# Codebook levels by masks and predicated copies in a transformer block: ScalarE makes the masks, VectorE picks the levels

## The reference

```
lora_delta = lora_B @ lora_A * 0.5                  # 512 x 512, rank 64
cb         = codebook / max|codebook|               # 8 levels
wg         = (weight + lora_delta) / scale          # scale = exp(scale_log), one per row and group of 128
idx        = searchsorted((cb[:-1] + cb[1:]) / 2, wg, side='left')
w_eff      = cb[idx] * scale + lora_delta
h = x @ w_eff.T
q, k, v = split(h @ Wqkv + bqkv)                    # 128 columns each
x = x + softmax(q k^T / sqrt(128)) v @ Wo + bo
base   = x @ W.T ;  logits = x @ Wr.T + 5 * onehot(language)
gates  = softmax of the top 2 of 8 logits
lora   = sum over experts of gate * (x @ A_e.T) @ B_e.T
x = x + (base + 2 * lora) @ (ffn_scale * (qweight - zero_point)).T + bias
```

## Time and profile before

| | before |
|---|---|
| median of three runs | 127.43 us (126.71, 127.43, 127.72) |
| profiled execution, first to last instruction (its span) | 125.8 us |
| TensorE busy | 104.7 us, 83% of the span |
| VectorE busy | 87.4 us, 69% |
| GpSimd busy | 53.7 us, 43% |
| ScalarE busy | 52.3 us, 42% |
| mean granted TensorE clock | 0.946 of full speed |

### The profile page before, as it was taken

How to read it: one execution, slowest core, us unless ns; L and a number is a source line. 1 busy time by engine, 2 the same in 40 slices (tenths; PEclk the granted TensorE clock), 3 DMA queues, 4 the chain that set the end, 5 groups by cost and what they waited for, 6 DMA issues and landing times.

```text
span 125.8 us, 1487 instructions
## 1 busy us (share of the span) xinstructions
PE 104.7 (83%) x512; PEld 88.5 (70%) x512; DVE 87.4 (69%) x162; ACT 52.3 (42%) x112; POOL 53.7 (43%) x52
## 2 busy tenths in 40 slices
...
GB/s 122 254 264 391 404 393 417 190 3 0 0 0 0 0 3 0 0 0 0 0 0 5 0 0 0 0 0 8 0 0 0 0 113 220 0 5 0 0 244 93
DMA packets 5512, 9.84 MB, mean 78 GB/s; under 512 B 768, under 2 KB 2048, under 8 KB 5504
## 3 DMA queue, kind: packets, MB, share of 16 engines
...
...
## 4 chain that ended last, share of the span: by engine, by line
PE 45%; DVE 35%; issue 7%; DMA 5%; SPq 3%; ACT 2%
DVE cond_work L709 14%; PE psum L916 13%; PE psum L917 12%; PE psum L918 12%; DVE cond_work L718 12%; DMA cond_n<-in_cond_w 5%; SPq L292 3%; DVE cuts L670 2%; PE psum L937 2%; DVE cond_work L774 2%; PE psum L1065 1%; PE psum L1044 1%; PE psum L1059 1%; ACT moe L472 1%; DVE split_b_lo L680 1%
## 5 line engine op out<-in xcount | busy, mean ns | idle before, releaser
L709 DVE TENSOR_SCALAR cond_work<-cond_n,cuts,rises 128x1024 f32<-128x1024 f32 x13 | 18.8, 1479 | 0.0
L718 DVE TENSOR_TENSOR cond_work<-cond_work 128x1024 f32<-128x1024 f32 x9 | 15.4, 1729 | 0.1
L916 PE MATMUL psum<-G_hi,xT_hi 128*128 128x512 f32 x32 | 12.9, 402 | 1.1 <-POOL xT_lo L531 1.1
L596 POOL TENSOR_TENSOR hl<-hl,hl_bias 128x272 f32<-128x272 f32 (+2 forms) x4 | 3.5, 886 | 22.5 <-ACT hl L364 14.6
L916 PE MATMUL psum<-wqkv_hi,split_a_hi 128*128 128x384 f32 x16 | 6.4, 402 | 8.1 <-DVE split_a_lo L780 8.1
L918 PE MATMUL psum<-G_hi,xT_lo 128*128 128x512 f32 x32 | 12.5, 390 | 0.0
L917 PE MATMUL psum<-G_lo,xT_hi 128*128 128x512 f32 x32 | 12.5, 390 | 0.0
L531 POOL TENSOR_TENSOR xT_lo<-xT,xT_hi 128x1024 fp32r<-128x1024 f32 x4 | 9.9, 2494 | 3.4 <-ACT xT_hi L337 3.4
L531 POOL TENSOR_TENSOR split_a_lo<-moe,split_a_hi 128x512 fp32r<-128x512 f32 x4 | 6.3, 1576 | 10.7 <-ACT split_a_hi L337 10.6
L916 PE MATMUL psum<-split_b_hi,split_a_hi 128*128 128x512 f32 x16 | 7.1, 443 | 4.1 <-DVE split_b_lo L680 4.1
L916 PEld LDWEIGHTS psum<-wqkv_hi,split_a_hi 128*128 128x128 f32 x16 | 3.8, 235 | 8.5 <-issue 8.5
...
## 6 DMA issues: line engine op xcount, KB each, us to landing
...
```

Source lines behind the costliest of these rows:

```text
L596: alone(pool.tensor_tensor(hl[:, t, :], hl[:, t, :], hl_bias[:, :].unsqueeze(1).to_broadcast([P, len(ts), HL]), ALU.add))
L709: ins = dve.tensor_scalar(half(dst, h), half(cond_n, h), cuts[:, j:j + 1], rises[:, j:j + 1], ALU.is_gt, ALU.mult)
L718: added[h] = mark(dve.tensor_tensor(half(acc, h), half(acc, h), half(step, h), ALU.add))
L916: pe.matmul(out_ap, l_hi, r_hi, start=first, stop=False)
```

## The change: what it does

- **Levels.** GpSimd fills `level` (the old `acc`) with the lowest level, two copies of 128x1024. For each cut and half ScalarE writes a mask, `beyond_cut`: Relu((value - cut) x 2^40), which is zero up to the cut, into one of two buffers. VectorE's `pick` is a predicated copy: where the mask isn't zero it writes the next level over `level`. Mask n waits for pick n-2, pick n for mask n and pick n-1. `cut_at`, `cut_add`, `cut_sum`, `delta_low`, Sign and Relu go.
- **FFN weight.** `w_full` makes scale x (q - zero_point) on VectorE in place, `w_hi` rounds it on ScalarE, `w_lo` is the rest on VectorE. So G and Bf need no further factor.
- **G, Bf, woG.** The identity is added by four small matmuls (`ident_r`) in PSUM. ScalarE rounds straight from PSUM, and VectorE subtracts straight from PSUM (`G_rest`, `Bf_lo`, `woG_lo`); GpSimd's part of this goes. `bo_G` is summed from eight terms and no longer four.
- **delta** is a plain fp32 matmul with 64 partitions, with no splitting ahead of it.
- **Loads** come in another order; half as much of lora is loaded. The small VectorE instructions that sort the cuts all stand ahead of `w_delta(0)` and end in `cut_bias`, which the masks need.
- **Orders.** `x_hl(2)` writes bank 5 (before: bank 1) and woG bank 0 (before: bank 5). The rounding of the second xT pair (`x_hi(1)`) stands behind mask 1 of half 1. On TensorE `y_x(1)` comes ahead of `y_x(2)`, and `y_x(3)` between the M steps of tiles 1 and 2.

```diff
-            load("lora_b", lora[:, 0, :], lora_in[:, 0, :])
-            load("lora_a", lora[:, 1, :], lora_in[:, 1, :])
+            load("lora", lora[:, :, :], lora_in[0:RANK, :, :])
+            load("hlT", hlT[:, :, :], hl_t)
             load("small", small[:, :], small_in)
-            load("hlT", hlT[:, :, :], hl_t)
             load("x_first", xT[:, 0, :, 0:SEQ], x_t[0, :, :, 0:SEQ])
-            load_proj_weights(0)
             load("x_second", xT[:, 0, :, SEQ:PT], x_t[0, :, :, SEQ:PT])
             load("cond_w0", cond_n[:, 0:2, :], cond_w[:, 0:2, :])
+            load_proj_weights(0)
+            load("x1", xT[:, 1, :, :], x_t[1])
             load_proj_weights(1)
-            load("x1", xT[:, 1, :, :], x_t[1])
             load("cond_w1", cond_n[:, 2:4, :], cond_w[:, 2:4, :])
...
+            load("exp_b", expb[:, :, :], exp_b)
             load("woT", woT[:, :, :], wo_t)
-            load("exp_b", expb[:, :, :], exp_b)
+            load("wqkv", wqkv_n[:, :, :], wqkv)
             load("x2", xT[:, 2:4, :, :].rearrange("p h t n -> p h (t n)"), x_t[2:4].rearrange("h p t n -> p h (t n)"))
-            load("wqkv", wqkv_n[:, :, :], wqkv)
...
+                n = nth(j, h)
+                if (j, h) == (0, 0):
+                    act.wait_ge(norm_first_ready, 1)
+                    act.wait_ge(cut_bias_ready, 1)
+                elif j == 0:
+                    act.wait_ge(norm_ready, GROUPS // 2)
+                if n >= 2:
+                    act.wait_ge(picked, n - 1)
+                act.activation(half(beyond, n % 2), half(cond_n, h), ACT.Relu, bias=cut_bias[:, j:j + 1], scale=CUT_GAIN)\
+                   .then_inc(beyond_ready, 1)
...
+            w_hi(0)
+            beyond_cut(0, 0)
+            beyond_cut(1, 0)
+            moe_hi(1)
+            w_hi(1)
             hl_raw(0, 4)
...
+            beyond_cut(2, 0)
             x_hi(0)
...
-            q_hi(3)
+            w_hi(2)
+            beyond_cut(3, 0)
             moe_hi(3)
+            w_hi(3)
+            hl_raw(1, 5)
+            beyond_cut(4, 0)
             normalise(1)
+            beyond_cut(5, 0)
             act.wait_ge(loaded["exp_b"], 16)
             rounded(expb_hi[:, :, :], expb[:, :, :], expb_hi_ready)
+            beyond_cut(6, 0)
             act.wait_ge(loaded["woT"], 16)
             rounded(woT_hi, woT[:, :, :], woT_hi_ready)
-            hl_raw(1, 5)
...
+                rounded(G_hi[:, i, :], psum[i][:, :], G_hi_ready)
...
+            act.activation(Bf_hi[:, :], psum[7][:, :], ACT.Copy, scale=EXPERT_SCALE).then_inc(Bf_hi_ready, 1)
             for o in range(CT):
-                rounded(wqkv_hi[:, o, :], wqkv_n[:, o, :], wqkv_hi_ready)
+                wqkv_round(o)
+                beyond_cut(2 + o, 1)
+            hl_raw(2, 5)
             act.wait_ge(woG_done, 1)
...
+            rounded(woG_hi, psum[0][:, :], woG_hi_ready)
+            beyond_cut(6, 1)
+            w_eff_hi(2)
+            w_eff_hi(3)
...
+            pool.wait_ge(levels_ready, 1)
+            for h in range(HALVES):
+                pool.tensor_copy(half(level, h), levels[:, 0:1].to_broadcast([P, 2 * C])).then_inc(level_set, 1)
             for o in range(CT):
                 pool.wait_ge(moe_hi_ready, o + 1)
                 rest(split_a_lo[:, o, :], moe[:, o, :], split_a_hi[:, o, :], moe_split_ready)
-                if o == 1:
+                if o == 2:
                     x_lo(0)
...
+            def w_full(o):
+                dve.wait_ge(loaded[f"q{o}"], 16)
+                dve.tensor_scalar(w_ffn[:, o, :], q_i[:, o, :], zero_point, ffn_scal, ALU.subtract, ALU.mult)\
+                   .then_inc(w_ready, 1)
+
+            def w_lo(o):
+                dve.wait_ge(w_hi_ready, o + 1)
+                dve.tensor_tensor(split_b_lo[:, o, :], w_ffn[:, o, :], split_b_hi[:, o, :], ALU.subtract)\
+                   .then_inc(w_lo_ready, 1)
...
+            def pick(j, h):
+                n = nth(j, h)
+                dve.wait_ge(beyond_ready, n + 1)
+                if j == 0:
...
+                    dve.wait_ge(picked, n)
+                dve.copy_predicated(half(level, h), half(beyond, n % 2).bitcast(I32),
+                                    levels[:, j + 1:j + 2].to_broadcast([P, 2 * C])).then_inc(picked, 1)
...
+            def G_rest(i):
+                dve.wait_ge(G_hi_ready, i + 1)
+                dve.tensor_tensor(G_lo[:, i, :], psum[i][:, :], G_hi[:, i, :], ALU.subtract).then_inc(G_lo_ready, 1)
...
+            w_delta(0)
+            dve.wait_ge(wd_ready, 1)
+            dve.wait_ge(inv_scale_ready, 1)
+            dve.tensor_tensor(blocks(0), blocks(0), inv_scale[:, 0:GROUPS // 2].unsqueeze(2).to_broadcast(
+                [P, GROUPS // 2, P]), ALU.mult).then_inc(norm_first_ready, 1)
+            w_full(0)
+            w_lo(0)
+            pick(0, 0)
+            w_full(1)
+            pick(1, 0)
+            w_lo(1)
+            pick(2, 0)
+            w_full(2)
+            w_lo(2)
+            w_full(3)
+            pick(3, 0)
+            w_lo(3)
             w_delta(1)
-            qmz(2)
-            dve.wait_ge(dve_step, kept)
-            kept = keep(2, ALU.min, 3)
-            cut_add(0)
...
+            pick(4, 0)
+            pick(5, 0)
+            pick(6, 0)
             w_eff(0)
             w_eff(1)
+            pick(0, 1)
+            for i in range(CT):
+                G_rest(i)
             w_eff_lo(0)
-            dve.wait_ge(sum_ready, 2)
-            dve.wait_ge(above_ready, 2)
...
+            w_eff_lo(1)
+            pick(1, 1)
+            dve.wait_ge(Bf_hi_ready, 1)
+            dve.scalar_tensor_tensor(Bf_lo[:, :], psum[7][:, :], EXPERT_SCALE, Bf_hi[:, :], ALU.mult, ALU.subtract)\
+               .then_inc(Bf_lo_ready, 1)
+            for j in range(2, CUTS - 1):
+                pick(j, 1)
+            dve.wait_ge(woG_hi_ready, 1)
+            dve.tensor_tensor(woG_lo, psum[0][:, :], woG_hi, ALU.subtract).then_inc(woG_lo_ready, 1)
+            pick(CUTS - 1, 1)
             w_eff(2)
             w_eff(3)
...
+            dve.wait_ge(G_lo_ready, CT)
+            parts = [part[:, c, :].bitcast(F32) for c in range(CT) for part in (G_hi, G_lo)]
+            one = mark(dve.tensor_scalar(bo_G[:, :], parts[0], bo_col[:, 0:1], None, ALU.mult))
+            for n in range(1, 2 * CT):
                 dve.wait_ge(dve_step, one)
...
-            pe.wait_ge(lora_lo_ready, 2)
+            pe.wait_ge(loaded["lora"], 16)
             for o in range(CT):
-                pe.matmul(psum[o][:, :], lora_bT[:, o * P:(o + 1) * P], lora_a_hi[:, :], start=True, stop=False)
-                pe.matmul(psum[o][:, :], lora_bT[:, o * P:(o + 1) * P], lora_a_lo[:, :], start=False, stop=True)\
+                pe.matmul(psum[o][:, :], lora[:, 0, o * P:(o + 1) * P], lora[:, 1, :], start=True, stop=True)\
                   .then_inc(delta_done, 1)
...
+                    three(psum[i][:, :], split_a_hi[:, o, s], split_a_lo[:, o, s],
+                          split_b_hi[:, o, :], split_b_lo[:, o, :], o == 0, False)
                     if o == CT - 1:
-                        mm.then_inc(G_done, 1)
+                        pe.matmul(psum[i][:, s], ident_r[:, :], ident_r[:, :], start=False, stop=True)\
+                          .then_inc(G_done, 1)
...
-            x_hl(2, 1)
+            pe.wait_ge(hl_raw_ready, 2)
+            x_hl(2, 5)
...
                 pe.wait_ge(G_lo_ready, c + 1)
-                mm = three(psum[5][:, :], woT_hi[:, c, :], woT_lo[:, c, :], G_hi[:, c, :], G_lo[:, c, :],
+                mm = three(psum[0][:, :], woT_hi[:, c, :], woT_lo[:, c, :], G_hi[:, c, :], G_lo[:, c, :],
...
+            pe.wait_ge(hl_raw_ready, 3)
+            y_x(1)
+            pe.wait_ge(woHL_ready, 1)
             pe.wait_ge(xT_lo_ready, 2)
-            pe.wait_ge(woHL_ready, 1)
             y_x(2)
-            pe.wait_ge(woG_ready, 1)
-            y_x(1)
-            pe.wait_ge(Bf_ready, 1)
+            pe.wait_ge(woG_lo_ready, 1)
+            M_product(0)
+            M_product(1)
+            pe.wait_ge(Bf_lo_ready, 1)
             y_x(3)
-
...
+            M_product(2)
+            M_product(3)
```

More of the change, by code:

```diff
@@ L62, in block_kernel @@
     LORA_SCALE = 32.0 / 64.0
+    CUT_GAIN = 2.0 ** 40
     LANG_BIAS = 5.0
@@ L153, in block_kernel @@
         cond_work = sb("cond_work", [P, 2, CT, C])
-        acc = cond_work[:, 0, :, :]
-        step = cond_work[:, 1, :, :]
-        above = q_i[:, 2:4, :].bitcast(F32)
+        level = cond_work[:, 0, :, :]
+        beyond = cond_work[:, 1, :, :]
+        w_ffn = q_i[:, :, :].bitcast(F32)
         def place(ap, n):
@@ L331, in x_pair, with half, nth @@
             return slice(pair * PT, (pair + 1) * PT)
+        def half(ap, h):
+            return ap[:, 2 * h:2 * h + 2, :].rearrange("p t n -> p (t n)")
+        def nth(j, h):
+            return CUTS * h + j
         @block.scalar
@@ L366, in hl_raw @@
                                ACT.Copy).then_inc(hl_raw_ready, 1)
-            def delta_low(o):
```

(41 more changed lines are left out.)

270 lines of the change are left out of this document (49 added, 221 removed).

## The result

The changed kernel takes 129.03 us, median of four executions (128.79 to 130.29), beside 127.58 (126.71 to 127.94) for the kernel before; the ratio is 1.0126, 95% interval 1.0067 to 1.0184. The prediction was 129.9. The profiled execution took 128.79, of which the span is 126.7; the span before was 125.8.

The account below looks back on a forecast made before the run. VectorE's chain, which TensorE awaits ahead of M, was taken as the bound. M's end +2.2 and bo_G +0.3 make span 128.3, and 127.43 + 2.5 = 129.9 us; range 124.2 to 132.8, likeliest case 127.6 to 132.

Parts of the forecast that it names:

- step (7): Behind M: bo_G's four more additions, 3.1 us against 2.8 idle ahead of neg_max, cost +0.3; everything else stays.
- Step (1): Start: cond_w0 lands near 9.3 us in place of 11.51; w_delta(0) starts at 10.2, between 9.3 and 12.
- Step (2): Up to the first pick: a GpSimd stop 1.0, w_full(0), w_hi and the first mask; pick(0,0) starts at 15.9 us.
- Step (3): Up to w_lo(3): picks 4.6, w_full 1.35, w_lo 2.0, GpSimd stops 3.0 + 2.1; 13.05 us, ending at 28.95.
- the far rival: Slower: predicated copy dearer than an addition; each 0.1 us costs 1.1, from 0.2 it gives 132 and more; chance 0.10.
- Steps (4) and (5): VectorE stands still 2.4 us for normalise(1), xT_lo holds it until 45.4, and hl_raw(2), behind mask 5, comes at 54.75.
- Step (6): TensorE waits for hl_raw(2) until 54.75; 16.6 us queued, 2.2 lost to the clock; M ends at 73.55, +2.2.
- GpSimd does not stop a pick: Faster: picks run unstopped beside GpSimd; M ends at 70.05, 126.4 us, or 124.2 if the clock holds; chance 0.20.
- All early: Faster: start and stops at their low ends, clock holds, TensorE never waits long; 124.8 us; chance 0.15.
- ScalarE's masks: Rival: they become the bound; in half 1 mask and wqkv_hi take 1.6 us per cut against 1.21; a further +1.

Follow-up runs that it names:

- e2: The changed kernel with 28 more TensorE matmuls of 512 columns ahead of the wait for the third x_hl copy; 127.04 us, one execution.
- e1: The changed kernel with ScalarE's copy hl_raw(2) moved ahead of the masks of cuts 2 to 5; 125.6 us, 0.9881 of the kernel before.
- e3: e1 with y_x(3) ahead of the M step of tile 0 in place of between tiles 1 and 2; 122.27 us, 0.9568 of the kernel before.
- e6: The kernel before with GpSimd's subtraction for Bf_lo moved right behind that for woG_lo; 126.79 us, ratio 0.9902.
- e8: e4 without GpSimd's four subtractions for wqkv_lo, which is filled with zeros; 120.07 us, 0.9405 of the kernel before.
- e7: e4 with woG's rounding and rest behind pick(2,1) in place of pick(5,1); 120.18 us, 0.9399 of the kernel before.
- e4: e3 with masks 5 and 6 of half 0 and the rounding of exp_b ahead of normalise(1) on ScalarE; 120.45 us, 0.946 of the kernel before.

## Why the prediction held

**The sum.** Predicted: 2.5 us more, span 128.3. Measured: 1.45 more in the medians, span 126.7. The 1.6 are M's end (73.08 for 73.55, -0.5), bo_G (0.0 for +0.3), Bf_lo's stop in the tail (-0.6, for which step (7) had nothing) and -0.2 that I can't place. Against that, the time outside the span was a term put at no change, and it changed: it is 2.0 to 2.1 in the four executions of the changed kernel (1.96 to 2.17 in all its variants), and 1.74 to 1.87 in every execution of the kernel before that ran beside them. The 1.6 came from the span of one execution and the median of three. So the change costs another 0.25 us outside the first and last instruction; why isn't shown. With it, and with spans up to 128.3, 129.03 stands closer to 129.9 than the traced span does to 128.3.

**Step (1), right.** `w_delta(0)` at 9.88 for 10.2. Not the load but the sorting of the cuts held it, stopped by GpSimd's two copies (1.04 each). **Step (2), 1.2 too late:** pick(0,0) at 14.71 for 15.9. 0.3 is step (1)'s; the rest is that the stop fell on `w_lo(0)` (1.27 for 0.66), which ran beside the first mask, and the step had stop and mask one behind the other. **Step (3):** `w_lo(3)` ended at 28.21 for 28.95; that stretch was 0.45 longer than its sum. Its four picks, from start to start, cost 0.36 more, the three `w_lo` 0.07 more, two waits for ScalarE (0.70 and 0.17) were not in the sum, and the stops were 4.25 in place of 5.1. A pick took 1.36 and not 1.21, so the copy is dearer than an addition by 0.15, under the 0.2 from which the far rival would have decided. **Steps (4) and (5), right** but for the same 0.7: the pause 2.29 for 2.4, xT_lo's hold, pick(1,1) ended at 48.8 for 49.4, `hl_raw(2)` done at 53.98 for 54.75. That this came out so close is in part luck: on eleven picks the dearer copy is 1.0 to 1.6 us (0.09 from start to start, 0.15 in length), and the early start and the shorter stops took it back.

**Step (6), the core, right:** the wait, its place, the releaser and the queue behind it. The queued work took 16.7 for 16.6 (e2), the clock 2.4 for 2.2; the step's own working, 4.7 less 2.35, gives 2.35 and not 2.2. e1 shows by itself that this wait was the loss: without it 0.988 of before. VectorE's chain did get shorter: its last `w_eff_lo` ends at 61.53, against 67.07 before. The change gave that back to one copy behind a mask. With the wait gone, the place of `y_x(3)` is worth another 4.25 (e3), so this copy is not all that the new order loses.

**Step (7), wrong twice, both small.** The four more additions were 3.1 (0.79 apart), and found room: `neg_max` still waits 0.34 for TensorE. A cast ahead of them took 0.86 in the kernel before, beside GpSimd's `woG_lo` (its row: `72.54 0.86 DVE L801 CAST lang_f<-lang_i 128x8 f32<-128x8 int32 x1`), and takes 0.16 now that this subtraction is gone: 2.79 - 3.1 + 0.70 leaves 0.39, so nothing of the chain is touched. And "GpSimd's `Bf_lo` and `woG_lo` there were hidden and give nothing" is refuted, for `woG_lo` by that cast and for `Bf_lo` by e6: it stopped an instruction on the chain for 0.6. The row was in the trace of before: the same instruction takes 1.31 at 83.88, beside Bf_lo, and 0.69 for the next four batches, at 100.46.

**The rivals.** "GpSimd does not stop a pick" is refuted: 2.21 at 18.51 beside GpSimd's subtraction, and in e8 pick(1,1) takes 1.35 in place of 2.17 once the subtraction beside it goes. "All early" needed four short waits; the start was early by 1.2, but the stops were only 0.85 shorter in step (3), and the clock did not hold. ScalarE's masks were no bound: VectorE waited for them 2.7 in all, 2.29 of it the pause.

**What remains open.** The step from the changed kernel to e7, 129.03 - 120.18 = 8.9 us, is explained to some 0.6 us: the stretches give 3.4 (e1), 4.25 (e3), 1.5 (e4) and 0.35 (e7), together 9.5. Not explained are the 0.25 us outside the span, the rest of e6's gain, and what decides whether the clock falls behind one and the same wait.
